# A two-layer graph kernel: the opening in another order, the last norm on VectorE, and the last sums of exponentials added there

## The chip, the core and the metric

The kernel runs on one core of a Trainium2 chip. The metric is the device time of one execution in microseconds. Three runs of the kernel before took 357.5, 357.8 and 357.8 us, median 357.8; the execution that the profiler recorded took 357.57 us, of which 355.8 us is the span of the trace.

## The reference, cut to what matters

```python
h = relu(layernorm(x))                                   # x: 4096 x 64, float32
Wh, We = h @ W, entity_embs @ W                          # entities: 4096 x 64
scores = (Wh @ a1)[:, None] + (We @ a2)[None, :]         # 4096 x 4096
e = where(adj > 0, leaky_relu(scores, 0.2), -9e15)       # adj: 0/1, symmetric, ones on the diagonal, sparse
x = x + elu(softmax(e, axis=1) @ entity_embs + h)
h = relu(layernorm(x))
x = x + ((adj == 1) @ h + h)                             # so the diagonal counts twice
```

## The kernel before

**Data.** Features lie in rows: x is held as `xs`, 4 pairs of row blocks, each pair 128 partitions (two times 64 features) by 512 rows. The adjacency is transposed and cut into 64 chunks of 128 x 2048 that the POOL queue loads as int32 and stores as one-byte floats in `am`, 27 slots of two chunks; at most 11 loads are under way (`UNDER_WAY`), and the last 10 chunks reuse slots that later work has freed. SyncE's queue loads the entities, the constant matrices and `xs`. A load waits in POOL's program order, among POOL's small operations.

**First layer.** The 4096 target rows are cut into 5 blocks, two of 512 rows (single) and three of 1024. For each block there is a loop of steps, 16 for a single block and 32 for a wide one, 128 in all, each for a tile of neighbours (two tiles when the block is single). In one step

- VectorE makes `yp` (L909, 128 x 1024 float32, one of `YS` = 7 buffers) as a max and a sum of the row part `s8b`, the tile's scalar `t8neg` and the byte code `coded`, which holds the mask and a shift of each row. The codes of four steps are made by one pass over the masks (`put_codes`, L822);
- ScalarE takes the exponential in place (L676);
- TensorE multiplies with the entities (L1222, 8 records) and, once for every two steps (a batch), with ones for the denominators (L1245, 8 records into the bank `dens`). `pv_done` counts steps whose batch is done, and VectorE's step n waits for `pv_done` n - 6, so it can be 7 steps ahead.

The shift of a row needs a bound on its largest neighbour score. For it TensorE runs the masks against a table of powers (`biggest(b, k)`, L1029, 8 parts per block; the part k of a wide block needs two chunks); VectorE reads the sums into `gmax` (`read_sums`, L789 and L790), TensorE turns them (`turn`), VectorE takes the largest and computes the shifts (`largest`, `shifts`), and TensorE (`v_rows`, L1056) and ScalarE spread them to `vx`, which `put_codes` adds. This is done for block b + 1 while block b's steps run: `SUMS`, `READ`, `TURN`, `LARGEST`, `VROWS` and `VOUT` give the step numbers at which each engine has these pieces in its program.

**First norms.** Pairs 0 and 1 are centred by a matmul with the centring matrix (`centred_first`, L1151), squared on ScalarE (`squares_first`), summed on TensorE (`variance`, L976), copied by ScalarE (`variances_first`), put to the power -1/2 on POOL, spread by TensorE (`deviation`, L986) and applied on VectorE (`normed`, L727). Pairs 2 and 3 are centred and squared ahead of the loop, and the rest of them lies in the loop's first steps (`NORM`). Column sums of the entities (L1143, 8 places of two records) serve rows whose shift is none; their split into three parts is a chain of 12 small POOL operations. `s_cols` and `s_rows` make the row scores.

**Second layer.** When a pair has its attention, its second norm is made in the steps of the block after next (`FIN`): inverses of the denominators, `weighted`, the elu (`negatives`, `rows_on`, which ends with `c_ready`), centring (`centred`, L1098), square and relu on ScalarE, variance columns (L1104) and the turn into natural rows (L1107), POOL's power, the product (`normed_again`), and a split of h into three bfloat16 parts (`highs`, `rests`, `middles`, `lasts`, which ends with `h_ready`). Then 32 pieces (`ORDER`) of 48 matmuls each (`neighbours`, L1132) add up the neighbours; a piece stands in the loop from the step that `PIECE_AT` gives, 12 matmuls a step, and 18 pieces are in the loop, 14 behind it. Pieces on the diagonal need POOL to add the identity first (`own`). Those behind the loop are given out in 6, 7, 2 and the remaining tiles of 12 matmuls, with `spread`, `centred` and `variance_again` of the last pair between them; tiles that use the last pair's h come 24 tiles behind the loop's end.

Every engine's order is written out by hand: a wait holds up all that stands behind it on that engine.

```python
            dve.wait_ge(pv_done, n - YS + 1)     # VectorE, step n, from n = 7 on
            pe.wait_ge(exp_done, n + 1)          # TensorE, step n
```

Of the kernel before, what the change touches and what calls it, by code (L numbers as in the profile page):

```python
# [5 lines left out]
P = 128  # L6
# [17 lines left out]
HALF = 512  # L24
# [30 lines left out]
PIECE_AT = (50, 51, 64, 67, 72, 78, 83, 84, 89, 93, 97, 100, 104, 108, 112, 116, 120, 124)  # L55
# [7 lines left out]
def graph_layers(nc, adj_t, xt, ent, w_t, a_cols, eye, out, N, M, D):  # L63
# [78 lines left out]
    def landed_of(q):  # L142
# [11 lines left out]
    SROWS = [None, 2, 20, 14]  # L154
# [4 lines left out]
           dict(den=2, comb=None, back=None, inv=5, bc=4, t=8, e=7, c=8, xc=8, sq=8, var=9, vs=10, hi=13, r=14, mid=14, lo=14)] * (NP - 2)  # L159
# [5 lines left out]
    NORM = {2: dict(dev=3, h=8), 3: dict(dev=5, h=10)}  # L165


    COLS_AT = (13, 20, 22)

    ctx = ExitStack()  # L170
    with ctx:
# [143 lines left out]
        ld_x = sem("ld_x")  # L315
        landed = [sem(f"landed{k}") for k in range(2 * SLOTS)]
# [45 lines left out]
        exp_done = sem("exp_done")  # L362
        pv_done = sem("pv_done")
# [46 lines left out]
        def _(sp):  # L410
# [4 lines left out]
            sp.dma_start(xs[:], xt).then_inc(ld_x, 16)  # L415
# [6 lines left out]
        def _(pool):  # L422
# [21 lines left out]

            g.iota(krow, [[1, KC]], base=0, channel_multiplier=0,
# [9 lines left out]
            for q in range(4):  # L455
                load(q)
# [76 lines left out]
            for w in OWN[4:6]:  # L533
                own(w)
# [5 lines left out]
        def _(act):  # L540
# [125 lines left out]
            for p in range(2, NP):  # L666
                squares_first(p)
                variances_first(p)
            for n in range(STEPS_ALL):
# [7 lines left out]
                e.then_inc(exp_done, 1)  # L677
                if n == COLS_AT[-1] + 3:
                    s_cols(range(1, NP))
# [28 lines left out]
            squares(NP - 1)  # L708
            variances(NP - 1)
# [4 lines left out]
        def _(dve):  # L714
# [99 lines left out]

            def put_codes(b, u):
                U = unit_at(b, u)
                if u == 0:
                    dve.wait_ge(vx_ready, first[b + 1])
                t = 2 * tiles(b)
                if U:  # L820
                    dve.wait_ge(y_made, steps_of(U))
                v.tensor_tensor(coded[:].bitcast(U16).rearrange("p (t i) -> p t i", t=t),  # L822
                                am[:, slot_of[U]].bitcast(U16).rearrange("p (t i) -> p t i", t=t),
                                vx[:, pair(b) % 2, cols(b)].bitcast(U16).unsqueeze(1).to_broadcast(
                                    [P, t, width(b) // 2]), ALU.add).then_inc(coded_ready, 1)
# [35 lines left out]
            def normed_again(b):  # L861
                m, s = 2, 0
                dve.wait_ge(hn_ps, b + 1)
                dve.wait_ge(rstd_ready, b + 1)
                hh, at = natural(b)
                v.tensor_tensor(hh.rearrange("p (s c) d -> p c s d", s=m),
                                turned.rearrange("p (c s d) -> p c s d", c=SUB, d=D)[:, :, s:s + m],
                                rstd[:].rearrange("p (c s) -> p c s", s=2)[:, :, s:s + m].unsqueeze(3).to_broadcast(
                                    [P, SUB, m, D]), ALU.mult).then_inc(hh_ready, 1)
# [19 lines left out]
            normed(1)  # L889
            dve.wait_ge(eyeb_ready, 1)  # L890
            read_sums(0)
            largest(0, 0)
            shifts(0)
            put_codes(0, 0)
            for n in range(STEPS_ALL):
# [5 lines left out]
                if jt % SUB == 0:  # L901
                    dve.wait_ge(coded_ready, unit_at(b, c // 2) + 1)
# [9 lines left out]
                y.then_inc(y_made, 1)  # L912
                if jt % SUB == SUB - 1 and c + 1 < HALVES[b] * NQ:
                    put_codes(b, c // 2 + 1)
# [398 lines left out]
```

## Time and profile before

| | |
|---|---|
| median of 3 runs | 357.8 us (357.5 to 357.8) |
| profiled execution | 357.57 us, span 355.8 us |
| TensorE matmuls busy | 330.2 us, 93% |
| VectorE busy | 271.1 us, 76% |
| ScalarE busy | 205.2 us, 58% |
| POOL busy | 74.7 us, 21% |
| chain: TensorE / DMA / VectorE | 54% / 23% / 18% |

PE is TensorE's matmul side, PEld its weight loads, DVE is VectorE, ACT ScalarE, POOL GpSimd, SP SyncE. A busy share is an average over the whole span. The row of granted clock and the busy tenths are in 40 slices of 8.9 us:

```profile
PE   1499689999969999999999999999999999999996
DVE  1753888999999999989998699999893998042201
PEclk9999969999999999999999999999999999999999
DMA  6999999999999999057005840000000000000011
```

TensorE has its idle time in the first six slices and some in the twelfth, the DMA engines are busy up to the sixteenth slice, and VectorE is nearly full from the fifth to the twentieth. The ends of matmuls are modelled, and a group that stands alone is shown some 0.2 us longer than what it costs in a row of groups.

### The profile page before, as it was taken

Reading aid. Unit: us, or ns where it says so; the run is one execution under the profiler, and the core shown is the slowest. Engines: PE = TensorE matmul, PEld = TensorE weight load, DVE = VectorE, ACT = ScalarE, POOL = GpSimd, SP = SyncE. Lnnn points to the kernel's source line nnn. Section 1 sums busy time; section 2 is a strip of 40 time slices with the busy share of each in tenths; the row PEclk is TensorE's granted clock in tenths of the full one; section 3 lists DMA queues with packets and bytes.
Section 4 is the critical chain, followed back from the end, with each engine's and each line's share of the span. In section 5 each row is a group of like instructions: output and inputs, shape, how many; then the busy total and the mean of one; then the engine's idle time right before and its main releaser. Section 6 shows DMA issues by size and latency. Waiting matters only on the chain.

```text
span 355.8 us, 8316 instructions
## 1 busy us (share of the span) xinstructions
PE 330.2 (93%) x3665; PEld 132.8 (37%) x3665; DVE 271.1 (76%) x334; ACT 205.2 (58%) x266; POOL 74.7 (21%) x118
## 2 busy tenths in 40 slices
PE   1499689999969999999999999999999999999996
PEld 1266324233322332342333334433343333345553
DVE  1753888999999999989998699999893998042201
ACT  1111594679768889557857885585748687032000
POOL 5463398212212030032002400000006000003000
PEclk9999969999999999999999999999999999999999
DMA  6999999999999999057005840000000000000011
GB/s 181 194 107 108 107 108 108 108 108 108 108 107 108 108 107 107 10 48 72 2 2 51 85 45 2 3 2 2 0 2 2 2 2 2 2 2 2 2 61 61
DMA packets 10419, 20.83 MB, mean 59 GB/s; under 512 B 1232, under 2 KB 1296, under 8 KB 10128
## 3 DMA queue, kind: packets, MB, share of 16 engines
q0 software_dynamic: 9216, 16.78, 47.5%
q1 hardware_dynamic: 1168, 3.52, 2.7%
q8 instruction: 29, 0.48, 0.5%
q14 instruction: 6, 0.05, 0.0%
HBM read 69.58 MB, written 1.05 MB: 199 GB/s over the span
## 4 chain that ended last, share of the span: by engine, by line
PE 54%; DMA 23%; DVE 18%; issue 2%; POOL 1%; ACT 1%; SPq 0%; DVEq 0%
DMA am<-adj_t 21%; PE pb L1222 17%; PE pb L1132 13%; DVE yp L909 11%; PE pa L1132 9%; PE pb L1245 8%; DMA mats<-eye 2%; DVE coded L822 2%; PE pa L1098 1%; PE pa L1104 1%; PE pa L1029 1%; POOL am L443 1%; DVE um L796 1%; PE pa L1006 1%; PE pa L1094 1%
## 5 line engine op out<-in xcount | busy, mean ns | idle before, releaser
L676 ACT ACTIVATE yp<-yp,tbias,delta 128x1024 f32<-128x1024 f32 (+1 forms) x160 | 162.1, 1066 | 42.9 <-DVE yp L909 42.6
L909 DVE SCALAR_TENSOR_TENSOR yp<-s8b,t8neg,coded 128x1024 f32<-128x1024 f32 (+1 forms) x160 | 162.6, 1072 | 3.0 <-PE pb L1245 1.9
L1222 PE MATMUL pb<-yp,enta 128*32 128x512 f32 x1024 | 132.3, 603 | 2.8 <-ACT yp L676 2.6
L1245 PE MATMUL pb<-yp,onesf 128*32 128x512 f32 x512 | 67.5, 600 | 0.0
L1132 PE MATMUL pb<-am,h 128*32 128x512 fp8e4 x960 | 60.9, 379 | 0.0
L443 POOL DMA_DIRECT2D am<-adj_t x64 | 34.9, 555 | 108.6 <-DMA am<-adj_t 55.1
L1222 PEld LDWEIGHTS pb<-yp,enta 128*32 128x32 f32 x1024 | 29.9, 111 | 58.1 <-issue 31.7
L1132 PEld LDWEIGHTS pb<-am,h 128*32 128x32 bf16 x960 | 28.0, 97 | 43.6 <-issue 29.3
L822 DVE TENSOR_TENSOR coded<-am,vx 128x2048 uint16<-128x2048 uint16 x32 | 40.0, 1249 | 2.5 <-ACT vx L568 1.1
L1132 PE MATMUL pa<-am,h 128*32 128x512 fp8e4 x576 | 34.9, 379 | 0.0
L505 POOL TENSOR_SCALAR rstd<-rstd 128x8 f32<-128x8 f32 x4 | 1.9, 463 | 132.9 <-ACT rstd L609 132.9
L1245 PEld LDWEIGHTS pb<-yp,onesf 128*32 128x32 f32 x512 | 16.4, 111 | 24.4 <-issue 18.2
L1132 PEld LDWEIGHTS pa<-am,h 128*32 128x32 bf16 x576 | 16.4, 97 | 22.7 <-issue 12.5
L1029 PE MATMUL pa<-am,gtab 128*32 128x512 fp8e4 x256 | 21.7, 399 | 2.7 <-DMA am<-adj_t 2.7
L1029 PEld LDWEIGHTS pa<-am,gtab 128*32 128x32 bf16 x256 | 6.8, 97 | 19.8 <-issue 16.4
L840 DVE TENSOR_TENSOR rows<-rows,rs 64x512 f32<-64x512 f32 x3 | 2.1, 689 | 11.6 <-ACT rs L583 11.5
L874 DVE TENSOR_TENSOR rs<-rs,h 128x512 f32<-128x512 f32 x4 | 3.7, 926 | 8.4 <-ACT h L626 8.4
L514 POOL TENSOR_TENSOR am<-am,eyeb 128x512 fp8e4<-128x512 fp8e4 x8 | 9.7, 1230 | 0.0
L558 ACT ACTIVATE s8b<-pa,delta 128x512 f32<-128x512 f32 x8 | 5.0, 681 | 7.5 <-PE pa L1006 7.4
L582 ACT COPY rows<-pb 64x512 f32<-64x512 f32 x3 | 1.7, 581 | 12.8 <-PE pb L1245 12.7
L954 DVE SCALAR_TENSOR_TENSOR yp<-pa,xs 128x512 f32<-128x512 f32 x2 | 1.4, 692 | 10.0 <-PE pa L1132 10.0
L568 ACT CAST vx<-pa 128x512 uint8<-128x512 f32 x8 | 4.3, 576 | 8.1 <-PE pa L1056 8.1
(165 smaller groups left out, 232.9 us busy)
## 6 DMA issues: line engine op xcount, KB each, us to landing
am<-adj_t POOLq DMA_DIRECT2D x64, 256.0 KB, 24.8
enta<-ent SPq DMA_DIRECT2D x1, 1040.0 KB, 5.5
xs<-xt SPq DMA_DIRECT2D x1, 1024.0 KB, 11.8
out<-yp SPq DMA_DIRECT2D x4, 256.0 KB, 2.0
mats<-eye SPq DMA_DIRECT2D x1, 320.0 KB, 7.3
num<-w_t SPq DMA_DIRECT2D x1, 32.0 KB, 2.1
a_sb<-a_cols SPq DMA_DIRECT2D x1, 0.5 KB, 2.0
```

What stands on the lines that cost most here:

```text
L443: pool.dma_start(am[:, slot, at:at + CHUNK], adj_t[q]).then_inc(landed[landed_of(q)[0]], 16)
L514: g.tensor_tensor(e, e, eyeb[:].unsqueeze(1).to_broadcast([P, SUB, P]), ALU.add, saturate=False).then_inc(own_ready, 1)
L558: sc.activation(s8b[:, p % 2, i * HALF:(i + 1) * HALF], bank_s(i), ACT.Copy, scale=delta[:, 1:2]).then_inc(s8_ready, 1)
L568: sc.copy(vx[:, pair(b) % 2, at:at + HALF], bank_s(i)).then_inc(vx_ready, 1)
L676: e = sc.activation(y, y, ACT.Exp, bias=tbias[:, at:at + 1], scale=delta[:, 0:1])
L822: v.tensor_tensor(coded[:].bitcast(U16).rearrange("p (t i) -> p t i", t=t), am[:, slot_of[U]].bitcast(U16).rearrange("p (t i) -> p t i", t=t),
L874: v.tensor_tensor(hh, hh, h3[:, at, 0:D], ALU.subtract).then_inc(rest_ready, 1)
L909: y = v.scalar_tensor_tensor(out=yp[:, n % YS, r * HALF:r * HALF + W], in0=s8b[:, pair(b) % 2, cols(b)], scalar=t8neg[:, at:at + 1], in1=c ...
L1029: mm = t.matmul(pa[g * KC:(g + 1) * KC, first[b] % 2 + i], gtab[:, jt], am[:, slot, at:at + HALF], start=(k == 0), stop=(k == NQ - 1), til ...
L1132: mm = t.matmul(gather(v)[at:at + 32, :], h3[:, jt, k * D + d:k * D + d + 32], masks(v, i, s), start=(v in OPENS and i == 0 and k == 0), s ...
L1222: t.matmul(acc2(b)[k:k + 32, :], enta[:, at, d:d + 32], yp[:, n % YS, s * HALF:(s + 1) * HALF], start=(jt == 0), stop=final, tile_position ...
L1245: mm = t.matmul(dens[at:at + 32, :], onesf[:, 0:32], yp[:, (m + r) % YS, s * HALF:(s + 1) * HALF], start=(opens and m + batch == n + 1), s ...
```

## The change

**Constants.** One piece fewer stands in the loop (17, so 15 behind it); two others move by one step. The sums of the later blocks, the reads and what follows them move by a few steps. `s_rows` of pair 1 comes at step 0 of its block, not at step 2.

```diff
-PIECE_AT = (50, 51, 64, 67, 72, 78, 83, 84, 89, 93, 97, 100, 104, 108, 112, 116, 120, 124)
+PIECE_AT = (50, 52, 64, 67, 72, 78, 83, 84, 89, 93, 97, 100, 104, 107, 112, 116, 120)
-    SUMS = [None, (0, 0, 0, 0, 1, 0, 3, 4), (7, 9, 12, 14, 15, 18, 20, 22), (30, 30, 32, 38, 40, 42, 48, 52),
-            (58, 62, 67, 68, 76, 78, 80, 84)]
-    READ = [None] + [s[-1] + 3 for s in SUMS[1:]]
+    SUMS = [None, (0, 0, 0, 1, 2, 3, 5, 6), (7, 9, 12, 14, 15, 18, 22, 23), (30, 30, 32, 38, 39, 43, 41, 52),
+            (58, 62, 67, 68, 76, 78, 80, 85)]
+    READ = [None] + [s[-1] + 4 for s in SUMS[1:]]
-    SROWS = [None, 2, 20, 14]
+    SROWS = [None, 0, 20, 14]
...
-    NORM = {2: dict(dev=3, h=8), 3: dict(dev=5, h=10)}
-    COLS_AT = (13, 20, 22)
+    NORM = {2: dict(sq=0, var=1, vs=1, dev=4, h=8), 3: dict(sq=2, var=2, vs=3, dev=6, h=10)}
+    COLS_AT = (12, 19, 24)
+    SUM_IN = [STEPS_ALL - YS, STEPS_ALL - YS + 1]
```

In `FIN`, `hi` of pairs 1 and 2 goes from 13 to 12.

**Loads.** Chunk 0 is loaded ahead of POOL's first small operations. `xs` comes in two halves, the second after the last chunk of block 0 has landed.

```diff
-            sp.dma_start(xs[:], xt).then_inc(ld_x, 16)
+            sp.dma_start(xs[:, 0:2], xt[:, 0:2]).then_inc(ld_x, 16)
+            sp.wait_ge(landed[landed_of(chunk0[1] - 1)[0]], landed_of(chunk0[1] - 1)[1])
+            sp.dma_start(xs[:, 2:NP], xt[:, 2:NP]).then_inc(ld_late, 16)
...
+            load(0)
             g.iota(krow, [[1, KC]], base=0, channel_multiplier=0,
...
-            for q in range(4):
+            for q in range(1, 4):
                 load(q)
```

**Opening on TensorE and VectorE.** The parts of block 0's sums stand ahead of the second pair's deviation and of the column sums. The squares of pairs 2 and 3 go into the steps (ScalarE after steps 0 and 2, variances after 1 and 3). The first block's first codes are made in two halves, the second behind step 0 (the `codes` helper is `put_codes` over a part of the tiles).

```diff
-            biggest(0, 3)
+            for k in range(3, NQ):
+                biggest(0, k)
             deviation(1)
-            for k in range(4, NQ - 1):
-                biggest(0, k)
-            column_sums(range(0, 2))
-            biggest(0, NQ - 1)
-            column_sums(range(2, 5))
             turn(0, 0)
-            column_sums(range(5, NT // 4))
+            column_sums(range(0, 4))
             v_rows(0, 0)
             biggest(1, 0)
+            column_sums(range(4, NT // 4))
             centred_first(2)
             centred_first(3)
             biggest(1, 1)
-            variance(2)
             biggest(1, 2)
-            variance(3)
...
             normed(0)
-            normed(1)
             dve.wait_ge(eyeb_ready, 1)
             read_sums(0)
+            normed(1)
             largest(0, 0)
             shifts(0)
-            put_codes(0, 0)
+            first_codes(0)
```

**The last four steps' denominators.** Their two batches go. VectorE adds `yp` of steps 124 and 125, and of 126 and 127, into two free buffers, and TensorE multiplies these two with ones behind step 127.

```diff
+                n = STEPS_ALL - 4 + 2 * r
+                dve.wait_ge(exp_done, n + 2)
+                dve.wait_ge(pv_done, SUM_IN[r] + (2 if SUM_IN[r] % 2 == 0 else 1))
+                v.tensor_tensor(yp[:, SUM_IN[r] % YS], yp[:, n % YS], yp[:, (n + 1) % YS], ALU.add).then_inc(y_summed, 1)
```

**The last norm.** For the last pair TensorE turns x itself (4 transposes) in place of centring it, making its variance columns and turning its relu; VectorE does the rest on the turned rows.

```diff
+            def rows_normed():
...
+                link(v.tensor_reduce(um[:], rows3, X, ALU.add))
+                link(v.tensor_scalar(um[:], um[:], 1.0 / D, None, ALU.mult))
+                link(v.tensor_tensor(t3, rows3, um[:].unsqueeze(2).to_broadcast([P, k, D]), ALU.subtract))
+                link(v.tensor_tensor(ta[:], tm[:], tm[:], ALU.mult))
+                link(v.tensor_reduce(um[:], ta[:].rearrange("p (k d) -> p k d", d=D), X, ALU.add))
+                v.tensor_scalar(rstd[:], um[:], 1.0 / D, None, ALU.mult).then_inc(var_sb, 1)
+                link(v.tensor_scalar(tm[:], tm[:], 0.0, None, ALU.max))
+                dve.wait_ge(rstd_ready, NP)
+                v.tensor_tensor(hh.rearrange("p (s c) d -> p c s d", s=2),
...
             spread(NP - 1)
             pieces(range(6, 13))
-            centred(NP - 1)
-            pieces(range(13, 15))
-            variance_again(NP - 1)
-            pieces(range(15, (len(ORDER) - PIECES) * SUB))
+            rows_turned()
+            pieces(range(13, (len(ORDER) - PIECES) * SUB))
```

ScalarE's `squares` and `variances` of the last pair go.

## Rows read from the trace of the kernel before

**Rows 1.** The chain of waits, in order of time: start us, us, what
```profile
63.02 26.75 DMA am<-adj_t
90.57 1.29 DVE gmax L789
...
190.91 1.13 PE pa L1098 x2
```

**Rows 2.** Timeline of the opening: start us, us, engine line op, [idle before <-releaser]
```profile
0.83 0.16 POOL L445 IOTA num<- 128x32 f32 x1 [0.40 <-POOLq L1305]
...
2.59 2.35 POOL L443 DMA_DIRECT2D am<-adj_t  x4 [0.31 <-POOL mhalf L453]
...
14.87 3.78 PE L1151 MATMUL pb<-xs,mats 128*128 128x512 f32 x4 [0.45 <-DMA xs<-xt]
...
28.74 0.40 PE L1029 MATMUL pa<-am,gtab 128*32 128x512 fp8e4 x4
...
30.09 0.83 PE L1029 MATMUL pa<-am,gtab 128*32 128x512 fp8e4 x12
...
30.83 0.53 POOL L443 DMA_DIRECT2D am<-adj_t  x1 [1.98 <-DMA am<-adj_t]
...
32.46 0.75 DVE L789 TENSOR_SCALAR gmax<-pa,wk 128x512 f32<-128x512 int32 x1 [1.55 <-PE pa L1029]
...
37.92 1.23 DVE L822 TENSOR_TENSOR coded<-am,vx 128x2048 uint16<-128x2048 uint16 x1 [1.11 <-ACT vx L568]
...
39.27 5.39 DVE L909 SCALAR_TENSOR_TENSOR yp<-s8b,t8neg,coded 128x512 f32<-128x512 f32 x8
```

**Rows 3.** The page, DMA queues: packets, MB, share of 16 engines
```profile
q1 hardware_dynamic: 1168, 3.52, 2.7%
```

**Rows 4.** Windows: busy us of PE, PEld, DVE, ACT, POOL; TensorE clock; DMA share; GB/s
```profile
2.00:3.00 1.00, 0.00 (x0) 0.00 (x0) 0.00 (x0) 0.00 (x1) 0.69 (x4) 1.00 0.16 33
46.00:48.00 2.00, 2.00 (x20) 0.39 (x14) 2.00 (x4) 2.00 (x4) 1.92 (x2) 0.50 1.10 114
```

**Rows 5.** Timeline, 42 to 105 us, of all engines
```profile
42.73 9.99 ACT L676 ACTIVATE yp<-yp,tbias,delta 128x512 f32<-128x512 f32 x14
...
45.42 0.62 PE L1029 MATMUL pa<-am,gtab 128*32 128x512 fp8e4 x4 [2.45 <-DMA am<-adj_t]
...
45.82 1.92 PE L1222 MATMUL pb<-yp,enta 128*32 128x512 f32 x8
...
47.53 2.77 POOL L471 TENSOR_SCALAR rstd<-rstd 128x8 f32<-128x8 f32 x1
...
51.60 1.58 DVE L909 SCALAR_TENSOR_TENSOR yp<-s8b,t8neg,coded 128x512 f32<-128x512 f32 x2 [1.38 <-PE pb L1245]
...
55.73 0.75 DVE L789 TENSOR_SCALAR gmax<-pa,wk 128x512 f32<-128x512 int32 x1 [1.29 <-PE pa L1029]
...
104.99 1.06 PE L1222 MATMUL pb<-yp,enta 128*32 128x512 f32 x8 [1.06 <-ACT yp L676]
```

**Rows 6.** The chain of waits from 300 us on
```profile
311.38 0.86 PE pb L1245 x8
312.24 3.89 PE pa L1132 x72
...
321.82 1.06 PE pa L1098 x2
...
324.29 0.98 PE pa L1104 x8
...
326.53 5.18 PE pb L1132 x96
```

**Rows 7.** Timeline of the tail, POOL and VectorE
```profile
325.56 0.20 POOL L505 TENSOR_SCALAR rstd<-rstd 128x8 f32<-128x8 f32 x1 [52.48 <-ACT rstd L609]
...
327.59 0.69 DVE L866 TENSOR_TENSOR rs<-pa,rstd 128x512 f32<-128x512 f32 x1 [6.18 <-POOL rstd L506]
...
330.85 0.69 DVE L879 TENSOR_TENSOR h<-rs,h 128x512 bf16<-128x512 f32 x1 [0.68 <-ACT h L631]
```

More of the change, by code:

```diff
@@ L532, in _ @@
                         own(w)
-            for w in OWN[4:6]:
-                own(w)
+            for w in OWN:
+                if PIECES <= w < OPENS[-1] + 2:
+                    own(w)
             deviations(NP - 1)
@@ L677, in _ @@
                 e.then_inc(exp_done, 1)
+                for p, f in NORM.items():
+                    if n == f["sq"]:
+                        squares_first(p)
+                    if n == f["vs"]:
+                        variances_first(p)
                 if n == COLS_AT[-1] + 3:
@@ L707, in _ @@
             negatives(NP - 1)
-            squares(NP - 1)
-            variances(NP - 1)
             highs(NP - 1)
@@ L813, in shifts, with codes @@
                 v.tensor_scalar(vb[:, 0:s], vq[:, 0, 0:s], NONE, None, ALU.add).then_inc(vb_ready, 1)
+            def codes(b, U, lo, hi):
+                t = 2 * tiles(b)
+                return v.tensor_tensor(coded[:].bitcast(U16).rearrange("p (t i) -> p t i", t=t)[:, lo:hi],
+                                       am[:, slot_of[U]].bitcast(U16).rearrange("p (t i) -> p t i", t=t)[:, lo:hi],
+                                       vx[:, pair(b) % 2, cols(b)].bitcast(U16).unsqueeze(1).to_broadcast(
+                                           [P, hi - lo, width(b) // 2]), ALU.add)
             def put_codes(b, u):
@@ L818, in put_codes, with first_codes @@
                     dve.wait_ge(vx_ready, first[b + 1])
[L819 to L825, printed above, removed]
+                dve.wait_ge(y_made, steps_of(U))
+                codes(b, U, 0, 2 * tiles(b)).then_inc(coded_ready, 1)
+            def first_codes(k):
+                if k == 0:
+                    dve.wait_ge(vx_ready, 1)
+                    link(codes(0, 0, 0, tiles(0)))
+                else:
+                    codes(0, 0, tiles(0), 2 * tiles(0)).then_inc(coded_ready, 1)
             def lone_rows(b):
@@ L1108, in variance_again, with rows_turned @@
                 mm.then_inc(hn_ps, 1)
+            def rows_turned():
+                pe.wait_ge(c_ready, NP)
+                for c in range(SUB):
+                    mm = t.transpose(turned[:, c * P:(c + 1) * P], xs[:, NP - 1, c * P:(c + 1) * P], eyef)
+                mm.then_inc(hn_ps, 1)
             def neighbours(v, i):
@@ L1225, in _ @@
                 for p, f in NORM.items():
+                    if n == f["var"]:
+                        variance(p)
                     if n == f["dev"]:
@@ L1233, in _ @@
                 batch = 4 if n >= FOUR_FROM else 2
-                if jt % batch == batch - 1:
+                if n == STEPS_ALL - 1:
+                    pe.wait_ge(y_summed, 2)
+                    for r in range(2):
+                        for s in range(2):
+                            at = r * D + s * 32
+                            mm = t.matmul(dens[at:at + 32, :], onesf[:, 0:32],
+                                          yp[:, SUM_IN[r] % YS, s * HALF:(s + 1) * HALF],
+                                          start=False, stop=True, tile_position=(0, at))
+                    mm.then_inc(pv_done, 4)
+                elif jt % batch == batch - 1 and n < STEPS_ALL - 4:
                     opens = jt == batch - 1
```

34 lines of the change are left out of this document (19 added, 15 removed).

## The prediction

> **What bounds the kernel now.** I read the chain of waits first. Up to 90 us it is the stream of 64 mask chunks, one after the other without a gap: the piece that starts at 63.02 ends at 89.77 with chunk 31, the last of block 2 [rows 1]. The reader is to see that VectorE's reading of block 2's sums follows 0.8 us behind it, that VectorE is the chain from there with one stretch of TensorE between, and that from 190.91 it is TensorE alone to the last outputs. Then the timeline of the opening. The first step (39.27) hangs on the first block's sums being read at 32.46 [rows 2]. Then the waits between 40 and 105 us: VectorE, which makes the 128 steps, waits there 1.38 us for TensorE's sums of exponentials and 1.29 us for the second block's mask sums, and both go back to one place: TensorE stood 2.45 us at 45.42 for a chunk [rows 5], after which its granted clock was 0.50, the 1.2 GHz level [rows 4]. So three queues are nearly full one after the other: DMA to 90, VectorE from 39 to 191, TensorE from about 100 to the end. A gain in the opening counts only as far as all three can take it.
>
> **The opening, part by part.**
> *First sums read.* Before them TensorE now has neither the second pair's deviation matmuls nor two column sums. From 28.74, where the columns of s end, five groups of 4 sum matmuls remain; 12 took 0.83 with a 0.2 tail [rows 2], so 20 take 1.25 and end at 29.99. The load of xs for pairs 0 and 1 is half as long, so its wait of 0.45 at 14.87 goes too, and what follows it on TensorE moves by that: 29.54, and the read starts at 29.6 instead of 32.46, 2.85 earlier. It needs chunk 7, which landed at 30.83 (the load that waited for it starts there). Two things bring that forward. Load 0 is issued at 0.83, where the first iota stands, not at 2.59 [rows 2]; the DMA engines were 0.16 busy from 2 to 3 us [rows 4], so the whole stream moves by 1.2 to 1.75; I take 1.5. And the second half of xs, 0.52 MB, goes behind chunk 7: the queue that moved 3.52 MB took 2.7% of 16 engines' 355.8 us [rows 3], 9.6 us, so 1.4. Chunk 7 lands at 27.9, in time. The moved half is wanted by TensorE near 37: hidden by 5 us or more. The small operations that load 0 passes on POOL start up to 0.6 later, under the wait for w1.
> *First codes in halves.* The pass took 1.23 [rows 2]; the first step now waits for half, 0.61 less; the split adds a fixed 0.1. The second norm fills the wait for the turn. First step: 39.27 - 2.85 - 0.61 = 35.8.
> *The two waits.* The sums of block 1 move from steps 0, 1, 0, 3, 4 (the third of these wanted chunk 13 before step 0's product) to 1, 2, 3, 5, 6; the 2.45 us stand goes, and the waits of 1.38 and 1.29 with it. Block 1's sums are now read after step 10, not 7: that is 3 steps of VectorE's work in which chunk 15 can land. What could be late next is ScalarE: 14 exponentials took 9.99 us, 0.71 each and 1.43 a step [rows 5], and the squares and variances of pairs 2 and 3 now stand among them (four passes of that size, 2.8 us, and an estimated 2 us of waiting for TensorE). By that step 7's exponential ends at 54 and step 8's turn on TensorE at about 57, where VectorE has the sums read. No queue waits above 1 us, and VectorE is at step 16 about 6.0 us earlier (3.45 + 2.67 - 0.1).
> *The second read.* Block 2's sums were read after step 25 at 90.57, after 0.26 of waiting; now after step 27, 3.97 of VectorE's work later (two steps 2.74, codes 1.23). VectorE would be there at 90.31 + 3.97 - 6.0 = 88.3. Chunk 31 lands at 89.77 - 1.5, and the read starts 0.8 behind it: 89.07. The old order would be there at 94.54. So here **the gain is 5.5 us and DMA sets it**: 4.0 with no earlier stream, 5.7 with 1.75.
> *Whether TensorE takes it.* It stands at step 23 for chunk 31 some 3.6 us, but the old wait of 1.06 at 104.99 [rows 5] falls away, and v_rows stands one product later, so that less work waits behind it. Counted from the read: vb 6.5 after it, at 95.6, then v_rows and the products and batches of steps 27 to 29: step 29's product, at 104.99 before, comes near 99.2, 5.8 earlier. From there the same work stands in the same order on the three queues. Moving one piece a step back (51 to 52) and the next read a step later costs nothing: TensorE, not the read, was late there; below nothing 0.5 is possible. The move of s_rows to step 0 of block 1 puts 1.06 of TensorE's work earlier that it had anyway; hi at 12 for 13 is ScalarE with idle time. Both: 0, bounds -0.3 to 0.3. VectorE leaves 190.91 5.5 us earlier, and TensorE then runs dense, as before.
>
> **The tail.** One piece (48 matmuls, 0.054 each by the row of 96 [rows 6], 2.6 us) moves behind the loop: TensorE's sum is unchanged. The last four steps' sums of exponentials: two batches of 8 records, 0.86 each [rows 6], become one group of 8: 0.86 goes. VectorE adds 128x1024 pairs for it, about 1.29 each by its pass over as many [rows 1]; the later one can start when the batch of step 123 is done, and TensorE then has four products of 0.86, 3.4, before it wants the sum: 2.1 us of cover; exposed whole it would cost 1.3. The norm: the centring product (1.06) and the variance columns (0.98) go, the 4 transposes stay: 2.04.
> Is h still there in time? Counted from the first piece behind the loop (312.24), TensorE needed h after 19.47, and it was there at 331.54 [rows 7], after 19.30 (0.17 of cover). Now TensorE needs it after 19.47 - 2.04 + 2.59 = 20.02. The new chain: x at 9.17, TensorE free for it at 9.58, transposes seen at 10.25; on VectorE a sum over rows, a scaling, a subtraction, a product, a second sum, a scaling: four at 0.72 (the like-sized L866 took 0.69 [rows 7]), two at 0.17: 13.5; POOL's two, as before from 325.56 to 327.59, 2.0: 15.5; product 0.79: 16.3; the two splits as before 3.26: **19.55, 0.47 ahead**. Bounds for the unseen row sums and broadcasts: 0.3 less and, with 2 us for all of them together, 1.5 more at the end.
> POOL's small operations are at risk beside VectorE: a 128x8 scaling took 2.77 us at 47.53 beside the steps [rows 5] and 0.20 at 325.56 [rows 7]. There a max on VectorE now runs beside POOL's pair. The Trainium skill (SBUF — State Buffer, "Who interferes with whom") says that a VectorE instruction with two SBUF inputs, or in a two-port mode, keeps GpSimd out for its whole length; the row of 47.53 agrees with that. By this rule POOL would wait for the max, at most 0.69 by the like-sized rows, the cover of 0.47 would be gone and the sum 0.2 smaller; without it nothing is lost.
>
> **Sum:** 5.5 + 0.86 + 2.04 = 8.4 us. The profiled execution took 357.57 with a span of 355.8, so 349.2; the median of the runs is 0.2 above it, so **349.4**.
>
> **Rivals.**
> *A, the early load moves nothing:* one chunk alone can't bring the stream forward, or POOL issues chunks 1 to 3 as much later. For it: the landing of chunk 31 is a chain of one transfer behind the other. Against: engines idle until 3 us. Opening 4.0: 357.8 - 6.9 = 350.9.
> *B, TensorE has no room:* it has few waits after 72 us, and if it loses half the opening's gain in its stand at step 23 and in the new order of block 0, the opening gives 2.8: 357.8 - 5.7 = 352.1. Against: its wait of 1.06, the stand of 2.45 and the low clock of before, all of which go.
> *C, the last norm is longer than its cover:* for it, six linked VectorE operations that no row shows as such; at 1.5 us over, 1.0 is exposed: 350.4.
> *D, slower:* the exponentials of block 0 are spaced by ScalarE's squares and its waits for variances, TensorE has gaps from 40 to 57 us and stays at the 1.2 GHz level through nearly the whole block. At that level 8 products took 1.92 us at 45.82 [rows 5]; 8 sums of that width take 0.86 at the high one [rows 6], and both levels carry a tail of 0.2; a step costs 1.3 more, and before about 5 steps ran so. All 16 at that level, with sums and turns, bring TensorE to step 16 some 11 us later than before; 3.6 come back at step 23's stand and 1.1 at the old wait, 2.9 in the tail: about 3 slower, 361. It decides from some 13 slow steps on. Against: new work fills the gaps and the long stand is gone. [...]
>
> **Numbers.** Forecast 0.50, A 0.17, B 0.17, C 0.10, D 0.06. The range takes the forecast's own bounds (gain 9.6 at most: opening 5.7 with 0.5 at the piece's place and 0.3 of the edits, tail 3.1) and reaches over A, C and B: 348.2 to 352.4; beyond it stand D and combinations of A to C. A measurement here tells 0.2% (0.7 us) from no change: faster 0.91, same 0.03, slower 0.06.
>
> **What would show it.** Chunk 7 landed before 29 and the first read at 29.6; the first step near 35.8; no TensorE wait for DMA before step 0 and no clock of 0.50 after 40 (D, if it lasts to 57); the read after step 27 at 89.1, within 1 us of chunk 31; TensorE in step 29's product near 99; an end of the loop about 9 us earlier (5.5 + 0.86 + the 2.6 of the piece); less than 0.1 us of wait before the pieces that need the last h; no wait at the last batch. The prediction is wrong if VectorE has new waits in block 0, or if TensorE lags the steps by all 7 buffers before 100 us.

## The result, and the profile after

The changed kernel takes 355.0 us (median of 5, 354.06 to 356.22), the kernel before 357.68 (357.5 to 357.8) beside it: ratio 0.9923 [0.9913, 0.9933]. It is faster by 2.7 us, and 349.4 with a range up to 352.4 was forecast. Its profiled execution took 355.18 with a span of 353.3. The page, busy times and the 40 slices:

```profile
PE 324.3 (92%) x3647; PEld 130.9 (37%) x3647; DVE 277.9 (79%) x344; ACT 204.1 (58%) x263; POOL 77.1 (22%) x118
...
PE   1189987899999989999999999999999999999996
...
DVE  0682897999999999999998789899984899455201
...
PEclk9995999999999999999999999999999999999999
```

TensorE's fourth slice (26.5 to 35.3) is at half clock; in the kernel before, that slice reads full and the sixth is low. VectorE's first slice is empty. The timeline of the opening, DVE, POOL and PE rows picked (start us, us, what, idle before and its releaser), answers to [rows 2]:

```profile
1.23 0.76 POOL L451 DMA_DIRECT2D am<-adj_t  x1 [0.80 <-POOLq L1355]
...
5.82 0.22 DVE L740 COPY num<-a_sb 64x128 f32<-64x128 f32 x1 [5.82 <-DMA a_sb<-a_cols]
10.86 2.29 DVE L743 TENSOR_TENSOR am<-enta,num 128x2048 f32<-128x2048 f32 x1 [4.82 <-DMA enta<-ent]
...
31.34 2.32 PE L1066 MATMUL pa<-am,gtab 128*32 128x512 fp8e4 x20
...
33.79 0.75 DVE L799 TENSOR_SCALAR gmax<-pa,wk 128x512 f32<-128x512 int32 x1 [6.30 <-PE pa L1066]
...
39.99 1.42 DVE L939 SCALAR_TENSOR_TENSOR yp<-s8b,t8neg,coded 128x512 f32<-128x512 f32 x2
```

VectorE's pass over the entities starts at 10.86; in the kernel before it started at 7.59. The first read of sums is at 33.79, 1.3 later than at 32.46 [rows 2], where 2.85 earlier was forecast, and the first step 0.7 later.

The windows of the opening (as [rows 4]) show the clock:

```profile
24.00:26.00 2.00, 1.90 (x20) 1.59 (x21) 1.63 (x10) 0.17 (x1) 1.83 (x3) 0.68 1.06 107
26.00:34.00 8.00, 7.76 (x48) 3.77 (x46) 0.90 (x2) 1.44 (x3) 5.53 (x10) 0.50 1.06 130
```

A granted clock of 0.50 is the 1.2 GHz level, so the 20 sum matmuls took 2.32 where 1.25 was forecast.

Block 0, answering to [rows 5]:

```profile
47.49 5.37 DVE L939 SCALAR_TENSOR_TENSOR yp<-s8b,t8neg,coded 128x512 f32<-128x512 f32 x8
47.74 5.19 POOL L480 TENSOR_SCALAR rstd<-rstd 128x8 f32<-128x8 f32 x1 [3.90 <-ACT rstd L657]
53.01 2.63 POOL L481 TENSOR_TENSOR rstd<-rstd,mhalf 128x8 f32<-128x8 f32 x1
55.70 1.09 PE L1023 MATMUL pb<-mats,rstd 128*64 128x128 f32 x16 [1.44 <-POOL rstd L481]
56.84 0.69 DVE L737 TENSOR_TENSOR h<-h,pb 128x512 f32<-128x512 f32 x1 [1.27 <-PE pb L1023]
60.98 0.69 DVE L737 TENSOR_TENSOR h<-h,pb 128x512 f32<-128x512 f32 x1 [0.60 <-PE pb L1023]
63.20 0.61 PE L1066 MATMUL pa<-am,gtab 128*32 128x512 fp8e4 x8 [2.27 <-DVE gmax L800]
66.16 0.69 DVE L806 TENSOR_REDUCE um<-pa 128x4 f32<-128x512 f32 x1 [0.47 <-PE pa L1078]
```

The old waits of 1.38 and 1.29 are gone, and 1.27, 0.60 and 0.47 stand in their place. The second read (block 2) starts at 95.16; by the prediction's count the old order without any change would have been there at 94.54. TensorE makes its rows of step 30 at 106.72 (before: 106.85) and its second block's centring at 191.09 against 190.91 [rows 1]. So **the opening gave nothing** in this execution: the whole gain is in the tail, which answers to [rows 6, 7]:

```profile
307.93 1.04 PE L1282 MATMUL pb<-yp,onesf 128*32 128x512 f32 x8
308.79 4.07 PE L1176 MATMUL pa<-am,h 128*32 128x512 fp8e4 x72
...
322.55 0.29 POOL L514 TENSOR_SCALAR rstd<-rstd 128x8 f32<-128x8 f32 x1 [47.91 <-DVE rstd L893]
322.93 1.65 POOL L515 TENSOR_TENSOR rstd<-rstd,mhalf 128x8 f32<-128x8 f32 x1
324.55 2.60 POOL L523 TENSOR_TENSOR am<-am,eyeb 128x512 fp8e4<-128x512 fp8e4 x2
324.68 1.51 DVE L896 TENSOR_TENSOR rs<-tm,rstd 128x512 f32<-128x512 f32 x1 [1.89 <-POOL rstd L515]
...
329.22 6.01 PE L1176 MATMUL pa<-am,h 128*32 128x512 fp8e4 x108 [0.25 <-DVE h L909]
```

One group of 8 for the last four steps, then the pieces. The last h is late by 0.25, because the product before it took 1.51 and not 0.69, beside POOL's own additions.

### The profile page after: what moved, and what is told of

It reads as the page before. It is cut to its first block, busy times and chain, and to the rows that moved or that the text cites. A ratio compares the mean times of both kernels' runs of the same rounds, so it can differ in the third digit from the quotient of the medians.

```text
span 353.3 us, 8289 instructions
## 1 busy us (share of the span) xinstructions
PE 324.3 (92%) x3647; PEld 130.9 (37%) x3647; DVE 277.9 (79%) x344; ACT 204.1 (58%) x263; POOL 77.1 (22%) x118
## 3 DMA queue, kind: packets, MB, share of 16 engines
HBM read 69.58 MB, written 1.05 MB: 200 GB/s over the span
## 4 chain that ended last, share of the span: by engine, by line
PE 50%; DVE 33%; POOL 4%; DMA 4%; issue 4%; ACT 3%; SPq 1%; DVEq 0%; POOLq 0%; ACTq 0%
DVE yp L939 19%; PE pb L1263 15%; PE pb L1176 10%; PE pa L1176 8%; PE pb L1297 7%; DMA xs<-xt 4%; DVE coded L827 4%; PE pb L1023 2%; PE pa L1066 2%; POOL rstd L480 2%; POOL rstd L481 1%; POOL rstd L515 1%; DVE um L806 1%; PE pb L1197 1%; DVE gmax L799 1%
## 5 line engine op out<-in xcount | busy, mean ns | idle before, releaser
L1263 PE MATMUL pb<-yp,enta 128*32 128x512 f32 x1024 | 130.8, 595 | 2.7 <-ACT yp L683 2.5
L1297 PE MATMUL pb<-yp,onesf 128*32 128x512 f32 x496 | 64.5, 592 | 0.0
L1263 PEld LDWEIGHTS pb<-yp,enta 128*32 128x32 f32 x1024 | 29.6, 109 | 57.7 <-issue 32.4
L827 DVE TENSOR_TENSOR coded<-am,vx 128x2048 uint16<-128x2048 uint16 (+1 forms) x33 | 41.4, 1255 | 2.5 <-ACT vx L578 1.1
L1176 PE MATMUL pa<-am,h 128*32 128x512 fp8e4 x576 | 33.8, 379 | 0.2 <-DVE h L909 0.2
L514 POOL TENSOR_SCALAR rstd<-rstd 128x8 f32<-128x8 f32 x4 | 2.7, 684 | 128.9 <-ACT rstd L619 81.0
L799 DVE TENSOR_SCALAR gmax<-pa,wk 128x1024 f32<-128x1024 int32 (+1 forms) x5 | 5.3, 1066 | 6.3 <-PE pa L1066 6.3
L606 ACT ACTIVATE tm<-ta 128x512 f32<-128x512 f32 x4 | 2.5, 630 | 11.2 <-DVE ta L873 11.2
L515 POOL TENSOR_TENSOR rstd<-rstd,mhalf 128x8 f32<-128x8 f32 x4 | 8.6, 2151 | 0.3
```

The lines of the kernel that those rows point to most:

```text
L515: g.tensor_tensor(rstd[:], rstd[:], mhalf[:], ALU.pow).then_inc(rstd_ready, 1)
L799: link(v.tensor_scalar(gmax[:, 0:W], sums, wk[:], None, ALU.min))
L827: return v.tensor_tensor(coded[:].bitcast(U16).rearrange("p (t i) -> p t i", t=t)[:, lo:hi], am[:, slot_of[U]].bitcast(U16).rearrange("p ( ...
L1176: mm = t.matmul(gather(v)[at:at + 32, :], h3[:, jt, k * D + d:k * D + d + 32], masks(v, i, s), start=(v in OPENS and i == 0 and k == 0), s ...
L1263: t.matmul(acc2(b)[k:k + 32, :], enta[:, at, d:d + 32], yp[:, n % YS, s * HALF:(s + 1) * HALF], start=(jt == 0), stop=final, tile_position ...
L1297: mm = t.matmul(dens[at:at + 32, :], onesf[:, 0:32], yp[:, (m + r) % YS, s * HALF:(s + 1) * HALF], start=(opens and m + batch == n + 1), s ...
```

## Experiments

"Changed" is the changed kernel; each edit is against the kernel named. All ratios are against the kernel before.

**1. Changed, with the first chunk loaded in its old place.**

```diff
-            load(0)
             g.iota(krow, [[1, KC]], base=0, channel_multiplier=0,
...
-            for q in range(1, 4):
+            for q in range(4):
                 load(q)
```

> The changed kernel with chunk 0's load back behind POOL's first small operations; all else as changed. Theory (the early chunk holds up the entity load and moves the stream by nothing): the entity pass on VectorE starts near 7.6 again instead of 10.86, the first sums are read near 30 to 31 and the first step is made near 36 to 37 instead of 39.99; chunk 31 lands within 0.3 of 89.8. The end comes 3.0 earlier or more than the changed kernel's: 351 to 352. Rival (the halved xs load delays the entities, and the early load is harmless): entities still near 10.9, time 355. Rival (the low clock from 24.5 to 35 is the loss, whatever the loads do): entities at 7.6 but clock 0.50 again near 25, first step after 38, time 353 to 354.

Measured: 352.45 (352.23 to 353.2), ratio 0.9859 [0.9846, 0.9872], 2.5 us faster than the changed kernel (experiment 10 limits what this figure says). Its opening:

```profile
3.34 0.22 DVE L739 COPY num<-a_sb 64x128 f32<-64x128 f32 x1 [3.34 <-DMA a_sb<-a_cols]
7.04 2.29 DVE L742 TENSOR_TENSOR am<-enta,num 128x2048 f32<-128x2048 f32 x1 [3.48 <-DMA enta<-ent]
...
29.83 0.75 DVE L798 TENSOR_SCALAR gmax<-pa,wk 128x512 f32<-128x512 int32 x1 [6.26 <-PE pa L1065]
...
32.13 3.32 PE L1186 MATMUL pb<-enta,onesf 128*128 128x260 f32 x8
...
37.06 1.42 DVE L938 SCALAR_TENSOR_TENSOR yp<-s8b,t8neg,coded 128x512 f32<-128x512 f32 x2
```

With the load back, the entities are there 3.8 earlier and the first read is at 29.83, near the 29.6 of the forecast. Not all of these 4.0 us are the load's. Here 16 of the 20 sum matmuls took 1.05, as at the high clock; in experiment 5, with the same loads, the 20 took 2.33 and the read came at 31.32, 2.5 earlier than in the changed kernel. The second read is at 92.33 here and at 92.07 in experiment 5, against 95.16. The first step is still 1.3 late, at 37.06: eight column-sum matmuls (L1186) took 3.32 at the low clock (0.50 from 32 to 34 us), and `v_rows` stood behind them. In experiments 6 and 8 the same eight took 1.92, and the first step was at 36.0, where 35.8 was forecast.

**2. The kernel before, with the early load alone** (the same two edits the other way round).

> The kernel before with the early load of chunk 0 alone. Theory: the entity pass starts near 10.9 instead of 7.59, the first step 2.5 to 3.5 later than 39.27, and, since block 2's sums are set by DMA with VectorE close behind, some of it is taken up: 1.5 to 3.3 us slower, 359.3 to 361. Rival (the early load as predicted, the stream 1.5 earlier): entities near 7.6 to 8, chunk 31 near 88.3, time 356.5 to 357. Rival (the halved xs is to blame): no delay here, 357.7.

Measured: 358.36 (357.53 to 359.91, 11 runs), ratio 1.0021 [1.001, 1.0032]. The rows:

```profile
10.78 2.29 DVE L734 TENSOR_TENSOR am<-enta,num 128x2048 f32<-128x2048 f32 x1 [4.86 <-DMA enta<-ent]
...
43.23 5.39 DVE L910 SCALAR_TENSOR_TENSOR yp<-s8b,t8neg,coded 128x512 f32<-128x512 f32 x8
...
91.75 1.28 DVE L790 TENSOR_SCALAR gmax<-pa,wk 128x1024 f32<-128x1024 int32 x1
```

The first step is 4.0 later, the second read only 1.2, the time 0.7: in the old order the waits of block 0 and the stream, which sets that read, take most of the delay back. In the new order it had less to hide in: there the second read is 2.8 later with the early load (95.16 against 92.33). The stream gained nothing here: POOL's load behind chunk 31 is at 90.17, and at 90.05 in the kernel before.

**3. The kernel before, with the three edits of the tail alone** (last norm from turned rows, the last steps' exponentials added on VectorE, one more piece behind the loop).

```diff
-            normed_again(NP - 1)
+            rows_normed()
...
+                if n == STEPS_ALL - 1:
+                    pe.wait_ge(y_summed, 2)
...
-108, 112, 116, 120, 124)
+108, 112, 116, 120)
```

> The kernel before with the tail's three edits alone: the last norm on VectorE from turned rows, the last four steps' exponentials added there, one piece behind the loop. Theory (the tail gives what its rows say): 0.86 + 2.04 less 0.25 of wait for the last h: 355.0 to 355.2. Rival (part of the changed kernel's 2.5 us came from the opening): 356 or more.

Measured: 354.97 (354.81 to 355.16), ratio 0.9926 [0.9913, 0.9939], 2.7 faster than before and level with the changed kernel whole. So the tail gave 2.65 of its 2.9, and by these medians the opening as changed is worth nothing.

**4. As 1, with the norm of pairs 2 and 3 two steps later**, against VectorE's wait at 56.84.

```diff
-dev=4, h=8), 3: dict(sq=2, var=2, vs=3, dev=6, h=10)}
+dev=6, h=9), 3: dict(sq=2, var=2, vs=3, dev=8, h=11)}
```

> As the first of these, and the spreading of pairs 2 and 3 moved from steps 4 and 6 to 6 and 8 on TensorE, the norm on VectorE from steps 8 and 10 to 9 and 11. Theory (POOL's 128x8 scaling, held up for 5.2 us beside VectorE's steps, is what TensorE and then VectorE wait for in block 0, 2.3 us in all): these waits shrink to under 1 us and step 16 comes 1 to 2 earlier than in the first; the time is 0.5 to 1.5 lower unless chunk 31's landing sets it. Rival (the waits are only moved: chunk 31 or ScalarE's order sets block 2's read): within 0.3 of the first.

Measured: 355.62 (354.58 to 355.89), ratio 0.9937 [0.9925, 0.9949]: 3.2 us slower than 1, a miss. VectorE's and TensorE's rows:

```profile
56.24 0.69 DVE L736 TENSOR_TENSOR h<-h,pb 128x512 f32<-128x512 f32 x1 [1.54 <-PE pb L1022]
59.78 1.04 PE L1065 MATMUL pa<-am,gtab 128*32 128x512 fp8e4 x8 [3.59 <-DVE gmax L799]
66.44 0.69 DVE L736 TENSOR_TENSOR h<-h,pb 128x512 f32<-128x512 f32 x1 [4.07 <-PE pb L1022]
```

Step 7's first mask sums of block 2 go into the PSUM half that the read of block 1's sums sets free, and that read now stands after step 10. TensorE stood 3.59 us for it, with pair 3's deviation matmuls (step 8) behind it, and VectorE then stood 4.07 us for those. Behind the stand the granted clock was 0.50 from 60 to 62 us, so the 3.2 are not the stand's alone. The stand of 2.27 at 63.20 in the changed kernel is the same one; there the deviations were ahead of it.

**5. As 1, with the sums of block 1 read after step 9.**

```diff
-    READ = [None] + [s[-1] + 4 for s in SUMS[1:]]
+    READ = [None, 9] + [s[-1] + 4 for s in SUMS[2:]]
```

> The changed kernel with chunk 0's load late, and block 1's sums read on VectorE after step 9 instead of 10. TensorE's first part of block 2's sums stands at step 7 and waits for that read (2.3 us in the changed kernel, the same banks). Theory: TensorE's stand before step 7 shrinks from 2.7 to about 1 us, but VectorE, which sets the pace there, loses nothing and gains at most its 0.5 us wait for the turn; the time is within 0.6 of 352.45, lower if anything. Rival (TensorE's lag is what costs in block 0): 1 to 2 lower, near 351.

Measured: 353.76 in the median, ratio 0.9874 [0.9852, 0.9895], on two levels: 351.94 and 351.99, and 353.76 to 353.89. In the profiled run, one of the lower two, the stand of 2.3 is gone, and TensorE stands 1.91 for a chunk at 75.87 instead. The clock column reads 1.00 throughout, yet the 20 sum matmuls took 2.33 at 28.88, as long as at 0.50 in the changed kernel; the second read is at 92.07. By its median the edit brings nothing; what decides between the levels is open.

**6. As 1, with the second POOL operation's input made by ScalarE:** its copy adds EPS for pairs 2 and 3, and POOL keeps only the power.

```diff
-                link(g.tensor_scalar(rstd0[:, p], rstd0[:, p], 1.0, EPS, ALU.mult, ALU.add))
+                if p < 2:
+                    link(g.tensor_scalar(rstd0[:, p], rstd0[:, p], 1.0, EPS, ALU.mult, ALU.add))
```

> The changed kernel with chunk 0's load late, and for pairs 2 and 3 the small epsilon added by ScalarE in its copy, so that POOL has only the power. Theory (POOL's scaling is locked out until VectorE's row of 8 step instructions ends, then the power follows for 2.6 us): the power starts with the end of the row near 50.0 instead of at 50.08 behind the scaling, or slightly before; if it is locked out itself and not only slowed, it ends near 51.6 to 52.7 and 0 to 1.1 us of VectorE's wait of 1.27 go: 351.4 to 352.4. Rival (the wait has another cause, ScalarE's or TensorE's order): no change of the waits.

Measured: 352.67 (351.79 to 353.52), ratio 0.9862 [0.9843, 0.9881]: as 1. Yet block 0 became shorter:

```profile
51.66 0.69 DVE L737 TENSOR_TENSOR h<-h,pb 128x512 f32<-128x512 f32 x1
55.80 0.69 DVE L737 TENSOR_TENSOR h<-h,pb 128x512 f32<-128x512 f32 x1 [0.60 <-PE pb L1023]
...
75.91 0.61 PE L1066 MATMUL pa<-am,gtab 128*32 128x512 fp8e4 x8 [2.72 <-DMA am<-adj_t]
...
77.31 1.96 PE L1297 MATMUL pb<-yp,onesf 128*32 128x512 f32 x8
```

The wait of 1.27 is gone, and step 16 comes at 69.84 instead of 72.10. Then TensorE stands 2.72 for chunk 25 in step 15, VectorE waits 1.19, 1.66 and 0.37 for it behind that, and the second read is at 93.46, 1.1 later than in 1. The 2.3 us, and 1.1 more, were given back in block 1. The clock has a part in it: behind the stand it was 0.50 from 78 to 80 us, and eight sums of exponentials took 1.96 where they take 1.04 at the full clock. Experiment 8 stood longer at the same group (3.35) with the clock at 1.00 behind it, and its read is at 92.03.

**7. As 1, with xs loaded whole** in front of chunk 7.

> The changed kernel with chunk 0's load late and xs loaded whole at the start. Theory (the later half brings chunk 7 forward by 1.4 us): chunk 7 lands at 30.8 instead of 29.3, the first sums are read at 31.3 instead of 29.83, the first step comes 0.8 to 1.4 later than 37.06 and the time is 0.7 to 1.4 higher than 352.45. Rival (the half makes no difference, as the entities and the clock set it): within 0.3 of 352.45.

Measured: 353.41 (351.95 to 354.05), ratio 0.988 [0.986, 0.99], about 1.0 slower than 1 by the medians, with intervals that overlap. The first read is at 32.06, 2.2 later than in 1, but only 0.7 later than in 5, where the 20 sum matmuls took 2.33 as they do here: 0.7 is the load's and the rest the clock's. The stream is faster behind it. POOL's load near 90 us, which waits for chunk 31, in the kernel before, the changed one, experiment 1 and this one:

```profile
90.05 0.53 POOL L443 DMA_DIRECT2D am<-adj_t  x1 [1.90 <-DMA am<-adj_t]
```

```profile
90.47 0.53 POOL L451 DMA_DIRECT2D am<-adj_t  x1 [1.93 <-DMA am<-adj_t]
```

```profile
90.72 0.53 POOL L451 DMA_DIRECT2D am<-adj_t  x1 [1.93 <-DMA am<-adj_t]
```

```profile
89.95 0.53 POOL L447 DMA_DIRECT2D am<-adj_t  x1 [1.88 <-DMA am<-adj_t]
```

So moving half of xs behind chunk 7 brought the chunks up to 8 forward by 0.7 (POOL's loads behind chunk 7 are at 29.55 against 30.26, behind chunk 8 at 31.95 against 32.67), not by 1.4, and put chunk 31 back by about 0.8. These are single executions; with the same loads the load behind chunk 31 lay between 90.68 and 91.12.

**8. As 6, with the read after step 9, and POOL's last additions held until the last h is made** (`pool.wait_ge(h_ready, NP)`).

> Chunk 0's load late, the read after step 9, epsilon on ScalarE, and POOL's last two additions of the identity held back until the last h is ready. The last is for the tail: the product over the rows took 1.51 us at 324.68 beside them, 0.69 expected, and TensorE then waited 0.25. Theory: that product takes 0.7 again, the wait of 0.25 goes, and with the others' gains the time is 350.7 to 352.0. Rival (the product is slow by itself, by its strided output): 1.5 again and no gain in the tail.

Measured: 352.99 (351.47 to 353.56, 4 runs), ratio 0.9864 [0.9845, 0.9884]. Step 16 is at 68.69, but TensorE stands 3.35 us for chunk 25 at 75.83, and the read is at 92.03. The product in the tail took 0.69.

**9. As 8, with two groups of mask sums later in block 1.**

```diff
-(7, 9, 12, 14, 15, 18, 22, 23)
+(7, 9, 12, 14, 17, 19, 22, 23)
```

> The kernel of the combined edits (first chunk loaded late, EPS on ScalarE, block 1's sums read after step 9, last additions held back), and in block 1 the fourth and fifth groups of mask sums at steps 15 and 17 instead of 14 and 15. Theory (what stops the gain of block 0 is TensorE's in-order queue: it stood 3.35 us at 75.83 for chunk 25 with the products of the next steps behind it): the stand falls below 1 us, VectorE's waits of 1.24, 1.04 and 0.65 for TensorE near 80 us go in the most part, TensorE is not at 1.2 GHz there, the read of block 2's sums comes at 90.5 to 91 where DMA alone sets it, instead of 92.03; 351.0 to 352.0 in the median (352.99 before), 350 to 350.5 with the full clock. Rival (the read is set by chunk 31 and nothing else, so the order of the groups does not matter): read within 0.3 of 92.0 and the time within 0.3 of 353.0. Second rival (the stand only moves to the next group, as TensorE must do the groups by chunk 31 anyway): a stand of 2 to 3 us at the group of step 17 or 19, same time.

Measured: 353.05 (352.84 to 353.06), ratio 0.9867 [0.9853, 0.988]. The second rival came nearest. The time is the same and there is a stand of 2.52, but at the last group (step 23); at step 17 TensorE does not stand, and at step 19 only 0.78:

```profile
67.21 0.61 PE L1067 MATMUL pa<-am,gtab 128*32 128x512 fp8e4 x8 [0.42 <-DMA am<-adj_t]
81.14 0.61 PE L1067 MATMUL pa<-am,gtab 128*32 128x512 fp8e4 x8 [0.78 <-DMA am<-adj_t]
90.97 0.61 PE L1067 MATMUL pa<-am,gtab 128*32 128x512 fp8e4 x8 [2.52 <-DMA am<-adj_t]
...
91.64 1.28 DVE L800 TENSOR_SCALAR gmax<-pa,wk 128x1024 f32<-128x1024 int32 x1 [1.18 <-PE pa L1067]
```

(The expectation says steps 15 and 17; the groups that moved are the fifth, 15 to 17, and the sixth, 18 to 19.) VectorE is in time for step 24, and both it and TensorE wait for chunk 31. 91.64 is the earliest read that the stream of this execution allows. And the time is not better than with a read at 92.3: TensorE comes out of the stand with the clock at 0.72 on the mean of 90 to 95 us, and turns the next sums late (VectorE waits 1.87 for them at 97.37).

**10. Changed, with only POOL's last additions held back**, as in 8.

> The changed kernel whole, with one edit: POOL's last additions of pieces (after its two operations for the last norm) wait until the last normed h is made. Theory (the product before h took 1.51 us instead of 0.69 because these additions run beside it, and TensorE waited 0.25 us for h): product 0.7, h 0.8 earlier, TensorE's wait before the pieces that need h gone, 0.25 faster: 354.75, and not more than that, since TensorE is the bound behind it. Rival (the row sum and product of that length are slow by themselves): product stays 1.5, no change. Second rival (the held additions are themselves wanted by the last pieces): a new wait of TensorE or VectorE for them at the end, 0.5 to 2.6 slower.

Measured: 352.77 in the median of 5, ratio 0.9863 [0.984, 0.9887]; its executions are 351.82, 352.54, 352.77, 354.39 and 354.78, the profiled one the last. In that one the tail did what the theory said: product 0.69, no wait of TensorE for h, and 354.78 against 355.18.

```profile
324.71 0.69 DVE L897 TENSOR_TENSOR rs<-tm,rstd 128x512 f32<-128x512 f32 x1 [1.89 <-POOL rstd L515]
```

An edit that acts behind 316 us, on a wait of 0.25, can hardly give the three runs 2 us below it. I take it that something ahead of the tail falls on two levels, as in 5, and that the changed kernel's five executions all lay on the upper one; those three runs left no trace, so this is not shown. It limits experiments 1 and 3: a kernel with the early load can also take 351.8 to 352.8, so the 2.5 us of experiment 1 is the difference between the executions compared, not a fixed price of the load, and the opening is worth nothing only on the upper level. What the load does to the rows, 3.8 us at the entities and 2.8 at the second read, is read from traces. So the size of this edit is read from the rows (0.25 to 0.4), not from the medians.

**11. As 1, with the order of 9 and the additions held back.**

> The changed kernel with the first chunk loaded late, the fourth and fifth groups of block 1 at steps 15 and 17, and the last additions held back; EPS stays on POOL and the read after step 10. Theory: with step 16 at 72.1 TensorE reaches the fifth group only shortly before chunk 25 lands (75.8), so the later place brings little here: 352.2, within 0.4 of 352.45, less the 0.25 of the tail. Rival (TensorE lags by a stand in block 1 here too): 351.3 or less.

Measured: 352.23 (351.38 to 352.54), ratio 0.9841 [0.9828, 0.9855], the best median of all, 5.4 faster than before and 2.8 faster than the changed kernel. Its interval overlaps that of 1, so it is not shown to be faster than that one.

## Why the prediction was wrong, step by step

*What bounds it* held. From the second read on the same work stood in the same order: by the 4.0 of later reading in the new order, 95.16 stands for 91.19 in the old, 0.6 later than before, and TensorE's place at 191 us was 0.2 later.

**The step that failed** is the early load: "Load 0 is issued at 0.83 ... so the whole stream moves by 1.2 to 1.75; I take 1.5", with nothing said of what it is put in front of. It went ahead of SyncE's a_sb and entities. a_sb was there at 5.82 instead of 3.34, the entities at 10.86 instead of 7.04, and the chain from them to the first codes moved by it. The Trainium skill (DMA: Bandwidth & Descriptors, "Queues, rings and completion order") says that a DMA engine takes turns between the queues that have work for it, a packet at a time; the delay of a 0.5 KB load from 3.34 to 5.82 fits that, though no run here tells this way of sharing from another. In the first 12 us the chunk queue moved 0.56 MB and SyncE's queue 1.33, against 0.37 and 1.87 in experiment 1. I had looked only at how idle the engines were. The stream got little in return: against experiment 1 the chunks near 41 us landed 0.7 earlier, and chunk 31 0.25. Experiments 1 and 2 show it from both sides: the second read 2.8 us later in the new order and 1.2 in the old, the median time 2.5 and 0.7 higher (the 2.5 with the reserve of experiment 10). The second read was forecast at 89.07 and came at 95.16. Of these 6.1 us, 2.8 go with the early load (92.33 without it in experiment 1; 92.07 in experiment 5, whose sum matmuls were as slow as the changed kernel's). About 2.2 more go with the stream: in experiment 1 its load at 90.72 allows a read from some 91.2 on (an estimate; in experiment 9 the read followed that load by 0.5). The last 1.1 is VectorE, which came to that read later than the stream. Rival A had the small gain right and the cost missing.

*xs in halves:* 1.4 forecast for chunk 7, about 0.7 by experiment 7; and the second half, "hidden", costs chunk 31 about 0.8. POOL's load behind chunk 31 is at 90.2 to 91.1, where by the forecast it would be at 88.6 (90.05 - 1.5). The earliest read was 91.64 in experiment 9, and by the load at 90.47 some 91.0 in the changed kernel (an estimate), so of the 5.5 us 2.9 to about 3.6 were there.

*The clock of the opening* had no place in the working. I took 1.25 for the 20 sum matmuls from rows at 2.4 GHz. In the changed kernel they took 2.32, with the clock at 0.50 from 26 to 34 us. The column of granted clock is no safe guide to this stage, and the durations are. In the kernel before, four sum matmuls took 0.62 at 25.16 and 0.40 at 28.74 [rows 2], and the column reads 1.00 for both:

```profile
25.16 0.62 PE L1029 MATMUL pa<-am,gtab 128*32 128x512 fp8e4 x4
...
24.00:30.00 6.00, 5.76 (x48) 3.36 (x44) 0.69 (x1) 1.33 (x3) 4.73 (x8) 1.00 1.06 106
```

In experiment 7 the 20 took as long as in the changed kernel, with the column at 1.00:

```profile
29.61 2.33 PE L1061 MATMUL pa<-am,gtab 128*32 128x512 fp8e4 x20
...
30.00:32.00 2.00, 2.00 (x22) 0.61 (x16) 0.00 (x0) 0.00 (x0) 0.54 (x1) 1.00 1.07 108
```

So by the durations the level was low there in the changed kernel and in experiments 4, 5, 7, 9, 10 and 11 (2.32 to 2.33 for the 20), and high in 1, 6 and 8 (1.05 for the first 16). This moves the first read by up to 1.5 us (29.83 in 1, 31.32 in 5) and is no matter of the early load, since 5 and 1 have the same loads. The Trainium skill (TensorE: Matmul & The Clock Gate, "The HAM clock gate") has the low clock as the resting state; the 0.62 of the first groups in the kernel before agrees. What made the changed kernel fall again is open: its groups took 0.40 at 22.96 and 24.28, TensorE was busy 1.90 of the 2 us from 24 to 26, and at 26.68 a group took 0.62.

*The waits of block 0:* "No queue waits above 1 us" was wrong. The old two went, as forecast. The new 1.27 has its source on POOL: its 128x8 scaling was issued 0.25 behind the start of a run of 8 step instructions of VectorE (two a step in this block) and ended with the run, 5.19 us later (before: 2.77, to the end of a run of 6). It ended with the run in experiments 1, 4, 5 and 7 too. I had costed ScalarE and TensorE in this chain, and had POOL's 2.77 before me, but asked of it only in the tail. The Trainium skill (SBUF — State Buffer, "Who interferes with whom") has GpSimd blocked for a whole instruction with two SBUF inputs; here it was shut out for eight in a row, 5.19 and not 0.7. Experiment 6 removes one of the two operations, and the wait with it. VectorE was to be at step 16 some 6.0 us earlier than the 74.01 of the kernel before; it was there at 75.03 in the changed kernel, 72.10 in experiment 1 and 68.69 in experiment 8.

*The later read of block 1* was counted as time for chunk 15, not as a PSUM half held three steps longer. TensorE stood 2.27 for it at 63.20; by its median experiment 5, without that stand, gains nothing; in experiment 4, with the deviations behind the stand and the clock at 0.50 after it, the time is 3.2 higher.

*Whether TensorE and DMA take the gain.* Where block 0 was made shorter (6, 8, 9), TensorE stood for a chunk in block 1, 2.5 to 3.4 us, and what follows on it stood too. That is rival B, at the place where the first group of sums meets a chunk that has not landed: step 15 in 6 and 8, step 23 in 9. Between step 16 at 68.7 and at 72.1 the time does not differ measurably.

*The tail* was right: 0.86 and 2.04 forecast, 2.65 measured. Missing is 0.25 of wait for h. Rival C had such a wait, but not its reason: not the new VectorE operations (row sums and broadcasts took 0.69 and 0.17, as taken), nor the max beside POOL's pair (0.42, with POOL's 0.29 beside it). POOL's additions started 0.13 ahead of VectorE's product and slowed it to 1.51. Experiments 8 and 10 show that.

Rival D did not come: after 36 us the clock was full.

**Open:** what puts whole executions of one kernel on levels some 2 us apart. In experiment 8 the clock goes with it (1.00 at 351.47, 0.981 to 0.985 at 352.8 and above); in experiment 10 it does not (0.990 at 351.82, 0.999 at 354.39). The mean clock of an execution says little here, as experiment 5 has 1.00 with its sum matmuls at the low level.

## What to carry to other kernels

Before a transfer is put into an idle gap of the DMA engines, look at which small loads it now runs beside, and who waits for them: one 256 KB chunk issued 1.3 us early cost 3.8 us on the load that the whole opening hung on. A small GpSimd operation on the path beside back-to-back VectorE work like these steps can cost the rest of that run of instructions (5.19 us for one of 0.20), so give it away or put it into a gap. And where three queues are nearly full, take a gain in one as an upper bound, and ask for the earliest time that the transfer stream allows before counting it. Hold the clock column against the duration of a group whose two levels are known, above all early in an execution.

## What the runs showed of the hardware

- POOL beside VectorE: 128x8 scaling 0.20 alone, 2.77 and 5.19 beside runs of 6 and 8 step instructions, ending with the run each time. The other way round, a 128x512 product of VectorE took 1.51 beside two additions of POOL that had started first, and 0.69 without them.
- With half of xs (0.52 MB) loaded beside the running chunk queue behind chunk 7, chunk 31 came some 0.8 later than with the same bytes loaded ahead of it (one execution without the move, 89.95, against 90.68 to 91.12).
- The same 20 sum matmuls took 2.32 to 2.33 in seven of the profiled executions, and the first 16 of them 1.05 in three, with nearly the same work before them. The clock column reads 1.00 in four of the seven slow cases (experiments 4, 5, 7 and 11).
- After stands of 2.5 to 3.6 us for a chunk or a PSUM half, the granted clock was 0.50 for some us in experiments 4, 6 and 9, and stayed at 1.00 in experiment 8 after one of 3.35.
